# A hybrid layer on one core: its two expert layers go from every expert for every token to lines sorted by expert, with weights picked by address

## What is computed

```python
x = x + L0_attn_a_ref(layernorm(x), ...)   # rotation of the head, one code vector a batch, RMS norm
x = x + L0_ffn_ref(layernorm(x), router_w, w1, w2)
x = x + L0_attn_b_ref(layernorm(x), ...)   # 16 heads of 8, 1,024 tokens a batch
x = x + L0_ffn_ref(layernorm(x), router_w, w1, w2)

# L0_ffn_ref: 8 experts, 256 hidden units, the best 2 experts of each token
logits = jnp.einsum('btd,ed->bte', x, router_w)
top_vals, top_idx = jax.lax.top_k(logits, K)
top_w = jax.nn.softmax(top_vals, axis=-1)
h = jnp.einsum('nd,edh->enh', xf, w1)
h = jnp.square(jax.nn.relu(h))
y = jnp.einsum('enh,ehd->end', h, w2)
y_sel = y[idx_f, jnp.arange(N)[:, None]]
out = jnp.einsum('nk,nkd->nd', w_f, y_sel)
```

## Time and profile before

| | |
|---|---|
| median of 3 runs | 1291.24 us (1288.02 to 1291.51) |
| profiled execution, its own time | 1291.25 us |
| its span, first to last instruction | 1289.5 us |
| PE busy | 1197.6 us, 93% |
| DVE busy | 976.4 us, 76% |
| ACT busy | 960.9 us, 75% |
| POOL busy | 285.5 us, 22% |
| mean granted clock of TensorE | 0.96 |

### The profile page before, as it was taken

The page is one execution under the profiler, slowest core; times in us unless marked ns, Lnnn a source line. Parts: engine busy times, 40 slices in busy tenths (PEclk is TensorE's granted clock), DMA queues, the critical chain, the costliest instruction groups (busy, mean ns, idle before and its releaser), DMA issues.

```text
span 1289.5 us, 25719 instructions
## 1 busy us (share of the span) xinstructions
PE 1197.6 (93%) x10019; PEld 742.1 (58%) x10019; DVE 976.4 (76%) x2357; ACT 960.9 (75%) x1826; POOL 285.5 (22%) x326
## 2 busy tenths in 40 slices
PE   1779999998899999999999999999999999999998
PEld 1369999987434434444444444444444348999998
DVE  7575677766888898989898888988889814565654
ACT  1037777765158998888898888988888996777775
POOL 2032000003423333332332333332322100000000
PEclk9679999999569999999999999999999999999999
DMA  5100000000000000000000000000000000000000
GB/s 193 36 1 1 1 1 1 2 1 1 1 1 1 2 1 2 2 1 2 2 2 1 2 2 1 2 1 2 1 2 1 1 2 1 9 17 9 10 9 17
DMA packets 6134, 11.08 MB, mean 9 GB/s; under 512 B 1907, under 2 KB 3574, under 8 KB 5878
## 3 DMA queue, kind: packets, MB, share of 16 engines
q1 hardware_dynamic: 6014, 9.45, 2.1%
HBM read 7.28 MB, written 2.10 MB: 7 GB/s over the span
## 4 chain that ended last, share of the span: by engine, by line
PE 78%; DVE 13%; ACT 6%; issue 3%; DMA 0%; SPq 0%; ACTq 0%; DVEq 0%
PE acc L1280 17%; PE six L1115 17%; PE six L1251 10%; DVE mxp L947 8%; PE six L1103 6%; PE six L1105 5%; PE six L1104 5%; PE misc L1251 5%; ACT PB L645 3%; PE six L1264 2%; PE six L1217 1%; ACT SC L634 1%; PE six L1127 1%; PE six L1212 1%; PE misc L1103 1%
## 5 line engine op out<-in xcount | busy, mean ns | idle before, releaser
L947 DVE TENSOR_REDUCE mxp<-six 128x2 f32<-128x1024 f32 x512 | 598.8, 1219 | 75.4 <-PE six L1264 73.4
L645 ACT ACTIVATE PB<-six 128x512 f32<-128x512 f32 x681 | 384.9, 599 | 60.7 <-PE six L1251 36.9
L1280 PE MATMUL acc<-PB,Vg 128*32 128x256 f32 x4096 | 328.0, 392 | 16.3 <-ACT SC L634 16.3
L1264 PE MATMUL six<-K,Q 32*128 32x512 f32 x1024 | 264.1, 519 | 14.4 <-DVE mxp L947 9.7
L1251 PE MATMUL six<-Q,K 32*128 32x512 f32 x681 | 272.5, 498 | 0.1
L1115 PEld LDWEIGHTS six<-w2s,PB 128*128 128x128 f32 x2048 | 248.2, 192 | 11.3 <-ACT PB L547 0.7
L1115 PE MATMUL six<-w2s,PB 128*128 128x128 f32 x2048 | 249.3, 275 | 0.1
L850 DVE SCALAR_TENSOR_TENSOR x<-six,wexp,x 128x128 f32<-128x128 f32 x512 | 144.2, 345 | 134.9 <-PE six L1115 134.2
L541 ACT ACTIVATE PB<-six 128x512 f32<-128x512 f32 x256 | 151.2, 599 | 114.8 <-PE six L1105 104.4
L645 ACT ACTIVATE PB<-misc 128x512 f32<-128x512 f32 x343 | 205.4, 599 | 23.2 <-PE six L1251 17.1
L1251 PEld LDWEIGHTS six<-Q,K 32*128 32x128 f32 x681 | 107.9, 183 | 142.7 <-ACT PB L645 73.4
(11 more groups left out here) (225 smaller groups left out, 1094.7 us busy)
## 6 DMA issues: line engine op xcount, KB each, us to landing
x<-in_x SPq DMA_DIRECT2D x4, 512.0 KB, 5.1
SC<-in_w_om SPq DMA_DIRECT2D x1, 2048.0 KB, 14.6
out<-x SPq DMA_DIRECT2D x8, 256.0 KB, 2.0
VH<-in_w SPq DMA_DIRECT2D x1, 1024.0 KB, 9.2
Vg<-in_wqs SPq DMA_DIRECT2D x1, 256.0 KB, 8.0
Vg<-in_wks SPq DMA_DIRECT2D x1, 256.0 KB, 7.4
cst<-in_cst SPq DMA_DIRECT2D x1, 81.5 KB, 3.4
nwb<-in_nw SPq DMA_DIRECT2D x1, 64.0 KB
```

The costliest lines, as they stand in the source:

```text
L645: act.activation(PB[:, s % 3, j, :], scores, ACT.Exp).then_inc(G_("act_taken"), 1)
L947: dve.reduce_max(dst, taken_slot("max", s, i).rearrange("p (a n) -> p a n", a=2), AX.X).then_inc(G_("max_taken"), 1)
L1264: ins = pe.matmul(slot[:, c * BLK:(c + 1) * BLK], Q[rows, G % NG, t * P:(t + 1) * P], K[rows, G % NG, th * BLK:(th + 1) * BLK], start=True ...
L1280: ins = pe.matmul(acc[RB * j:RB * (j + 1), n], Vg[:, G % 2, t, j, :], PB[:, s % 3, j, n], start=(t == 0 and half == 0), stop=(t == TPB - 1 ...
```

## The change

Both expert layers compute only the two chosen experts of a token. Per batch of 1,024 tokens:

- DVE normalises the 8 tiles into `hbs`, PE turns them (`turn_rows`) and multiplies by the router (`batch_router`), DVE finds the best two (`batch_top_two`), PE counts with a triangular matrix how many lines of each expert stand before each (`batch_rank`), and DVE makes of it a place for each of the 2,048 lines (`batch_places`), experts one after the other, each from a multiple of 128 on. That is at most `RT` = 23 tiles of 128 lines.
- POOL writes the lines to their places in device memory with 16 indirect transfers of 128 lines (`send`, L501). SP fetches them back in 6 groups of up to 4 tiles (`load_lines`, L443).
- PE turns the lines (`turn_lines`, L1443) after it has loaded 4 numbers into registers (L1437), multiplies each tile, as the stationary operand, by 256 columns of its expert's w1 at an address from a register (`lines_hidden`, L1454), turns the units that DVE rectified (`units_turned`, L1465), and multiplies those that ACT squared by w2 at an address from a register (`lines_result`, L1479). Tiles go in pairs, `PAIRS` = 12 a batch (the last has one tile); a pair's three steps are two pairs apart. w1 is no longer split and is loaded later.
- ACT copies the results, SP stores them (`keep_lines`, L450), and POOL gathers them in the order of the tokens with 16 indirect transfers a batch (`fetch`, L507). DVE adds them into x (`add_results`).

In the first layer batches 0 and 1 are routed ahead of all expert work, 2 and 3 beside the pairs of batches 0 and 1; results of batches 1 to 3 are fetched and added during the attention. In the second layer batches 0 to 2 are routed in the attention's last group (`routed_late`), 3 beside batch 0. `attention_end` now stands by itself ahead of `experts(1)`. Norm statistics that DVE took beside the first expert layer are taken in the attention (`late_stats`).

```diff
-RMS_GROUPS = ((0, 2), (2, 2), (4, 4))
+RMS_GROUPS = ((0, 2), (2, 2), (4, 2), (6, 2))
...
+RT = (2 * L + E * (P - 1)) // P
+TG = 4
+RGROUPS = -(-RT // TG)
+PAIRS = -(-RT // 2)
...
-            pl.tensor_copy(w1h[:], w1f).then_inc(G_("w1_split"), 1)
-            pl.wait_ge(G_("w1_split"), 1)
-            pl.tensor_tensor(w1l[:], w1f, w1h[:].bitcast(F32), ALU.subtract).then_inc(G_("w1_split"), 1)
...
+                for i in range(TPB):
+                    for k in range(2):
+                        pl.indirect_dma_start(xs[b], bass.IndirectOffsetOnAxis(ap=dest[:, b, k, i:i + 1], axis=0),
+                                              hbs[:, b, i, :], None).then_inc(G_(f"sent{b}"), 16)
...
             def experts(f):
-                if f == 0:
-                    pe.wait_ge(G_("wqk_loaded"), 48)
-                    pe.wait_ge(G_("w1_split"), 2)
-                    pe.wait_ge(G_("w2_loaded"), 16)
-                experts_block(f, 0, False, attention_end if f else None)
-                for n in range(1, NBLK - 1):
-                    experts_block(f, n, False)
-                experts_block(f, NBLK - 1, True, None if f else attention_start)
-                expert_out(NBLK * f + NBLK - 1, E - 1)
...
+                turn_lines(f, 0, 0)
+                for s in range(PAIRS * B):
+                    b, q = divmod(s, PAIRS)
+                    if q % 2 == 0 and s + 2 < PAIRS * B:
+                        turn_lines(f, *divmod(s // 2 + 1, RGROUPS))
+                    lines_hidden(f, b, q)
+                    if s:
+                        units_turned(f, *divmod(s - 1, PAIRS))
+                    if s >= 2:
+                        lines_result(f, *divmod(s - 2, PAIRS))
+                    route = routed_beside(f, b)
+                    if route and q in (5, 6):
+                        turn_rows(f, route, q - 5)
+                    elif route and q == 7:
+                        batch_router(f, route)
+                    elif route and q == 9:
+                        batch_rank(f, route)
...
+            for e in range(6):
+                attention_end(e)
             experts(1)
```

More of the change, by code:

```diff
@@ L450, in _ @@
             low_part(2, 0)
-            split_out(0, 0)
             low_part(2, 1)
-            for t in range(1, 4):
+            for t in range(4):
                 split_out(0, t)
@@ L459, in _ @@
                 split_out(1, t)
+            pl.memset(MX, 0.0).then_inc(G_("mx_zeroed"), 1)
+            fetch_start(0, 1)
+            for i in range(4):
+                fetch(0, 1, i)
             minus_max(0, 0)
@@ L463, in _ @@
             bias_block(1)
+            for i in range(4, 7):
+                fetch(0, 1, i)
             shift_queries(0, 0)
+            fetch(0, 1, 7)
             minus_max(0, 1)
@@ L470, in _ @@
                     split_out(G + 2, 0)
+                if b == 0:
+                    if g % 2 == 0:
+                        fetch_start(0, 2 + g // 2)
+                    for i in range(2):
+                        fetch(0, 2 + g // 2, 4 * (g % 2) + i)
                 if g < NG - 1:
@@ L481, in _ @@
                     split_out(G + 2, 2)
+                if b == 0:
+                    for i in range(2, 4):
+                        fetch(0, 2 + g // 2, 4 * (g % 2) + i)
                 if g < 2 and b < B - 1:
@@ new lines, in add_results @@
+            def add_results(f, b, u):
+                dve.wait_ge(G_(f"back{b}{u}"), 16 * TPB * (f + 1))
+                for k in range(2):
+                    for i in range(TPK * u, TPK * (u + 1)):
+                        xt = x[:, b * L + i * D:b * L + (i + 1) * D]
+                        ins = dve.scalar_tensor_tensor(out=xt, in0=lines_back[b][:, k, i, :],
+                                                       scalar=pw[:, b, k, i:i + 1], in1=xt, op0=ALU.mult, op1=ALU.add)
+                    if k == 0:
+                        link(ins)
+                ins.then_inc(G_("mixed"), 1)
@@ L1081, in _, with second_rows @@
             pe.wait_ge(G_("mg_ready"), 1)
-            for n in range(NBLK):
+            def second_rows(n):
                 if n == NBLK - 1:
@@ new lines, in batch_rank @@
+            def batch_rank(f, b):
+                pe.wait_ge(G_("both_ready"), sparse_index(f, b) + 1)
+                if f == 0 and b == 0:
+                    pe.wait_ge(G_("tri_ready"), 1)
+                rank, all_lines = route_bank(f, b)[:, 128:128 + TPB * E], route_bank(f, b)[:, 192:192 + E]
+                pe.matmul(rank, tri[:], both[:], start=True, stop=False, skip_group_check=True)
+                for d in range(1, TPB):
+                    pe.matmul(rank[:, d * E:], ones[:], both[:, 0:(TPB - d) * E], start=False, stop=(d == TPB - 1),
+                              skip_group_check=True)
+                for i in range(TPB):
+                    ins = pe.matmul(all_lines, ones[:], both[:, i * E:(i + 1) * E], start=(i == 0), stop=(i == TPB - 1))
+                ins.then_inc(G_("rank_done"), 1)
@@ new lines, in _, with turn_lines @@
+            expert_at = {}
+            def turn_lines(f, b, g):
+                n = RGROUPS * sparse_index(f, b) + g
+                pe.wait_ge(G_("tw_ready"), sparse_index(f, b) + 1)
+                pe.wait_ge(G_(f"line{g}"), 16 * (sparse_index(f, b) + 1))
+                if n:
+                    pe.wait_ge(G_("lines_stored"), n)
+                _, experts = nc.values_load_multi_w_load_instructions(
+                    tw[0:1, b, TG * g:min(RT, TG * (g + 1))], engines=[PE], min_val=0, max_val=HID * (E - 1),
+                    skip_runtime_bounds_check_because="VectorE bounds each of them when it writes them")
+                for i, at in enumerate(experts):
+                    r = TG * g + i
+                    expert_at[b, r] = at
+                    ins = pe.transpose(line_bank[:, i * P:(i + 1) * P], lines_in[b][:, r, :], ident)
+                ins.then_inc(G_("lines_turned"), 1)
@@ new lines, in lines_hidden @@
+            def lines_hidden(f, b, q):
+                n = PAIRS * sparse_index(f, b) + q
+                group = RGROUPS * sparse_index(f, b) + q // 2
+                pe.wait_ge(G_("lines_stored"), group + 1)
+                if n >= 2:
+                    pe.wait_ge(G_("rlp_done"), n - 1)
+                for r in range(2 * q, min(RT, 2 * q + 2)):
+                    ins = pe.matmul(big[:, n % 2, r % 2 * HID:(r % 2 + 1) * HID],
+                                    hTs[:, group % 2, r % TG * P:(r % TG + 1) * P], w1s[:, ds(expert_at[b, r], HID)],
+                                    start=True, stop=True)
+                ins.then_inc(G_("hidp_done"), 1)
```

709 lines of the change are left out of this document (478 added, 231 removed).

## The result

| | before | changed |
|---|---|---|
| median of 3 runs | 1291.24 us | 1479.32 us (1477.88 to 1484.84) |
| ratio, 95% interval | | 1.148 (1.142 to 1.153) |
| span of the profiled execution | 1289.5 us | 1476.1 us |
| PE busy | 1197.6 us | 1150.4 us |
| POOL busy | 285.5 us | 510.0 us |

A forecast was written before the change was run, and what follows sets the result against it. PE was taken to bound the expert layers, waiting for nothing. First maxima 29.8 us earlier and attention +37 gave 1074; attention_end +9, second layer 142, tail 27 gave 1252, with 1.75 outside the span 1254 us; range 1198 to 1318.

The forecast's parts named there:

- POOL's price: Indirect transfers on POOL: 1.1 us each, 17.6 for 16, landing 2.0; about 40 of them on the path.
- POOL's queue binds: Rival: at 2.2 us a transfer on POOL, 44 us more and some 20 of stalls, 1318 us; chance 0.09.
- the clock stays at half: Rival: in the expert layers, pairs with gaps keep the clock at half, 92 at 2.62 us more, 1495 us; chance 0.03.
- a step above 3.3 us: Sign in the expert layers that the forecast is wrong; steps of 2.8 to 2.9 us were expected in batches 2 and 3.
- the attention, +37 forecast: Attention: 7 first group, 6 norm statistics, 6 more additions, 18 last group; last product with values at 1074 us.
- Additions and statistics: DVE's extra attention work: +7 for two additions and delayed fetches, +6 norm statistics, +6 four more additions.
- Last group: Attention's last group: 20 us more PE work and 4 on ACT, all but 3 counting, with a wait for places: +18.
- Work on a pair of tiles: PE in the expert layers: results 0.89, hidden units 0.89, transposes 0.84, together 2.62 us a pair, 120.5 a layer.
- Addresses: Register addresses on PE: one 0.25 us gap a step, 12 us a layer; unhidden register loads would make the sum 28 higher.
- Layers: Expert layers: first 153 us, first maxima at 295.6 instead of 321.4; second 142 us.
- First routing: Before the first layer: norms, router, best two, rank, places, transfers and load; expert work starts at 130 instead of 93.4.
- Tail: After the second layer's last result: copy, store, 16 fetches 17.6, landing 2.0, additions and store: 27 us.

The follow-up runs named there:

- four_in_flight: Changed kernel with at most four transfers of a batch in flight and the second layer's batch 3 sends ahead of batch 0's fetches: 1302.6 us, 1.010.
- no_transfers: Changed kernel with all 256 indirect transfers replaced by POOL instructions that write one number and give the same signal: 1273.5 us, 0.985 of the kernel before.
- rank_by_prefix: four_in_flight with the rank in 6 records, DVE adding the counts of the tiles ahead: 1277.0 us, 0.989 of the kernel before.
- fixed_experts: four_in_flight with each tile's expert fixed in the program, so no register loads or register addresses on TensorE: 1298.3 us, 1.006 of the kernel before.
- two_in_flight: Changed kernel with each send or fetch beyond a batch's first two waiting until the transfer two before has landed: 1341.6 us, 1.038.

## Why the prediction was wrong

**Where it failed: "POOL's price".** That step asked what a transfer costs POOL and who waits for it to land, and took 1.1 us and 2.0. Both were near (1.25, and 2.2 to 2.6 to landing in four_in_flight). The row of the changed kernel for the fetches:

```profile
L507 POOL DMA_INDIRECT hbs<-yd,dest x96: 942/947/1018, 266.5 to 1465.7; - x96
```

0.95 us, and 0.30 between two: 1.25. It never asked what a row of 16 does to engines that have nothing to do with POOL, and so put that at nothing. That is the largest term of the miss: between the changed kernel and four_in_flight lie 177 us of the medians (174 of the spans), of which some belong to the new order on POOL. By stage they are 70 in the first layer's hidden products, 25 in the attention (of it 21 in the last group, which stands beside 48 sends) and 77 in the second layer. Of the rivals, "POOL's queue binds" came nearest by its cause, and went by the wrong mechanism: it had PE wait for transfers. The lines were there; the signals were not. By its number "the clock stays at half" came nearest, 1495 us, and that is luck: the mean clock of the two layers is 0.82 and 0.80, and 1.00 where POOL is done. Of the signs of being wrong, a step above 3.3 us did come (4.3 in the mean of the first layer, 137.9 to 343.6 us for 48 steps), but not by way of addresses. The Trainium skill (SBUF — State Buffer, Reading the diagram), which I had weighed there, says that some operations of DVE and GpSimd exclude each other at a shared port, so that transfers from GpSimd can starve. Here the transfers didn't starve: POOL kept 1.25 us in the middle of each hole, and PE, which by the same section never waits at that port, was the one held up. What the Trainium skill says there isn't contradicted by these runs; it just isn't what happened.

**The second failure: the attention, +37 forecast, +94 without any transfer (no_transfers: 757.1 + 82.3 against 745.4 before).** Two terms; the clock has a part in both.

- *Additions and statistics* (7 + 6 + 6 = 19). Measured 51. I charged DVE's extra time once, 2.3 us an addition and 1.2 for statistics. But a piece of 2.3 us on DVE, which is busy for 88% there, makes PE wait, and then the granted clock falls: 0.84 over 400 to 600 us, where the kernel before had 0.98 in the same groups, as its window shows:

```profile
366.00:560.00 194.00, 186.59 (x1807) 79.41 (x1807) 172.29 (x193) 170.22 (x321) 67.01 (x78) 0.98 0.01 1
```

  It is shown both ways: without that work the groups have their old length, and with all of it, cut into pieces, the clock is 0.96 and groups that were 58 us too long in rank_by_prefix are 38 too long.
- *Last group* (+18). Measured +43 without transfers. The term was 20 us of PE work at a full clock. PE was busy for 81.51 of 82.30 us, so there was no idle time to speak of, and the clock was 0.66. It stood at half from about 1062 us on for most of the rest, and the group's own work ran at that clock too. Six records instead of 32 for each batch's rank took 15 us off it. The Trainium skill (TensorE: Matmul & The Clock Gate, HAM oscillation) ties a falling clock to gaps in PE's work; the first term goes that way (in no_transfers from 400 to 600 us PE waits for DVE, up to 2.7 us at a time, at a clock of 0.85), the last group does not: no gaps in the records, 8 columns a record just before the fall, and 1.2 GHz for a good part of it.

**What held, and its size.**

- *Work on a pair of tiles*: 2.62 us forecast; the timeline of the changed kernel after the hole gives 2.19 us for a step without transposes of lines and 2.63 with four of them, 2.41 in the mean:

```profile
305.98 1.03 PE L1454 MATMUL six<-w1s,VH 128*128 x4
306.84 0.60 PE L1465 MATMUL six<-cst,PB 128*128 128x128 f32 x4
307.28 1.06 PE L1479 MATMUL six<-w2s,PB 128*128 x8
308.17 0.60 PE L1443 MATMUL six<-cst,Q 128*128 128x128 f32 x4
308.61 1.03 PE L1454 MATMUL six<-w1s,VH 128*128 x4
```

  0.86 us for hidden units (0.89 forecast), 0.44 for four transposes (0.56), 0.89 for results (0.89). The transposes were what I had too dear.
- *Addresses* (12 us a layer): nothing to see here, as no step has a gap, and fixed_experts takes 0.4 us off the first layer and 1.4 off the second. A load of registers takes 0.33 us in the row below, beside PE's work. The Trainium skill (DMA: Bandwidth & Descriptors, Latency and other measured facts) has a floor of about 600 ns for one; this kernel's loads are under it, and the 28 us that I had worked out from it are not there.

```profile
L1437 PEldq TENSOR_LOAD <-tw x48: 328/333/1604, 131.0 to 1430.1; - x48
```

- *Layers*: without late signals 151 us to the attention's first maxima (166 forecast) and 123 for the second (142). This is the gain that I had seen, 33 us more than I had said.
- *First routing*: the first hidden product at 137.9 instead of 126. Of the 12 us, 3 to 4 are a late signal: four_in_flight has 134.9, and in this row DVE waits for router products that PE had ended 4.4 us before. The rest is none: no_transfers has 134.1. rank_by_prefix is 5.7 us under four_in_flight, with 26 small records less a batch. Differences of this size between two traces are weak here: fixed_experts, the same program up to this point, has 140.5.

```profile
124.68 0.22 DVE L1078 COPY lgb<-six 128x64 f32<-128x64 f32 x1 [10.67 <-remote]
```

- *Tail*: 27 forecast, 32.7 measured. The rows: the first of the last 16 fetches, the last, and the last addition, 2.5 us behind the issue.

```profile
1446.87 0.94 POOL L507 DMA_INDIRECT hbs<-yd,dest  x1 [18.66 <-DMA yd<-PB]
...
1465.67 0.94 POOL L507 DMA_INDIRECT hbs<-yd,dest  x1 [0.30 <-issue]
1468.19 2.32 DVE L1132 SCALAR_TENSOR_TENSOR x<-hbs,pw,x 128x128 f32<-128x128 f32 x8 [7.59 <-DMA hbs<-yd,dest]
```

Taken together, the sum missed more than the two things above, and the other errors partly cancel: four_in_flight, where nothing is late, has a span of 1301.9 us where the sum said 1252, and that 50 us is the attention's +61 and the start's +9 and the ends' +12, less 33 in the layers.

**What stays open.** Why a row of more than 12 ready indirect transfers holds PE up, by way of which queue, and why PE far more than ACT and DVE. Only the kind of the transfers, the length of the row and what stands between them were told apart. How much of it is late products (the rows of 202.24 to 205.74 us) and how much late signals isn't known either. All executions here were recorded by the profiler, which writes down each instruction; whether a row of transfers costs the same where nothing is recorded was not tested. And why the clock falls in the attention's last group is open.

## What to carry to other kernels

When POOL issues indirect transfers beside work on TensorE, don't let more than a dozen stand ready in a row: put in a wait for the landing of a recent one. In two_in_flight that costs POOL nothing in the first 16 sends (19.3 us from first to last, 19.2 in four_in_flight) and 8 us in the first 16 fetches (26.7, where the changed kernel takes 18.8), and it was worth 138 us. A wait for something that landed long ago doesn't help. Charge an insertion on an engine that is near its limit with what its neighbour loses, clock included, and cut it into pieces that fit the slack of a step. Price a small record of TensorE at what it takes in a row at the clock that it will meet (0.22 us at half clock here), and count them. And if waits have a releaser that the profile can't name while every engine that they could come from has long been done, look at what a fourth engine does in that stretch.

## What the hardware did that I had not expected

- Indirect transfers of 128 lines in a row on POOL: 14 us of TensorE's time lost in a burst of 16, and signals up to 31 us late beside a row of 32. With 12 in a row, or 8 and 8 with a wait that holds, or a one-column memset between: 0. Plain transfers: 0 for 16 and for 40 in a row. Waits that were met long before change nothing.
- Beside such a row single products of TensorE, which wait for nothing in the program, come 1.4 and 2.1 us apart.
- TensorE busy for 99% of a stretch and the clock at 0.66, where records with 8 columns stand between others; with 78 small records fewer, 0.72.
- Addresses from registers on TensorE, six a pair, and a load of four registers every second step: no gap between products.
